# Edge features of a graph layer, by edge or by feature: four tiles per matmul, turned back through SBUF

## The reference

```python
h = maximum(layernorm(x), 0.0)                  # 6250 x 96
ea = edge_attr @ W_edge.T + b_edge              # 106250 x 96
msg = relu(h[src] + ea)                         # gather by source node
aggr = segment_sum(msg, dst)                    # scatter-add to 6250 nodes
h = (1.0 + eps) * h + aggr
h = relu(h @ W1.T + b1)
out = x + h @ W2.T + b2
```

## Time and profile before

| | before |
|---|---|
| median of 3 runs | 1239.65 us (1236.34 to 1239.94) |
| profiled execution, its span | 1239.1 us |
| its own time less the span | 0.55 us, if the median stands for it: no time of its own is given |
| TensorE matmul, weight load busy | 628.9, 515.6 us |
| VectorE, ScalarE busy | 518.5, 193.0 us |
| GpSimd busy | 785.9 us |
| bytes moved by DMA | 93.30 MB, mean 75 GB/s |

### The profile page before, as it was taken

The page is one execution under the profiler, slowest core; times in us unless marked ns, Lnnn a source line. Parts: engine busy times, 40 slices in busy tenths (PEclk is TensorE's granted clock), DMA queues, the critical chain, the costliest instruction groups (busy, mean ns, idle before and its releaser), DMA issues.

```text
span 1239.1 us, 9124 instructions
## 1 busy us (share of the span) xinstructions
PE 628.9 (51%) x2786; PEld 515.6 (42%) x2786; DVE 518.5 (42%) x658; ACT 193.0 (16%) x233; POOL 785.9 (63%) x838
## 2 busy tenths in 40 slices
PE   2226544455554454555554555444555545554568
PEld 2215434344433334444444444343444434443456
DVE  6645344444433333354344333333343444333373
ACT  5102111111111111111111111111111111111114
POOL 6756666666666666666666666666666666666540
PEclk9999666665656665565665656655556565565668
DMA  8513222333222223333333332222222333232212
GB/s 217 145 33 94 66 64 67 74 85 74 67 67 67 68 67 75 72 73 75 74 93 95 76 74 66 67 67 67 64 66 68 74 88 72 68 67 61 49 29 78
DMA packets 51183, 93.30 MB, mean 75 GB/s; under 512 B 17722, under 2 KB 20443, under 8 KB 51136
## 3 DMA queue, kind: packets, MB, share of 16 engines
q0 software_dynamic: 26592, 40.85, 16.3%
q1 hardware_dynamic: 24390, 51.63, 15.2%
q10 hardware_dynamic: 154, 0.24, 0.1%
HBM read 87.85 MB, written 4.80 MB: 75 GB/s over the span
## 4 chain that ended last, share of the span: by engine, by line
another core or an unknown queue 56%; DVE 23%; issue 8%; DVEq 8%; PE 3%; DMA 1%; ACT 0%; SPq 0%; ACTq 0%
DVE edge_ps L854 7%; DVE edge_ps L865 5%; DVE msg_parts L879 4%; DVEq L768 3%; DVE acc L759 2%; DVEq L770 2%; DVE acc L849 1%; PE edge_ps L601 1%; DVEq L762 1%; DVE stats L639 1%; PE edge_ps L462 1%; DVEq L795 1%; DVE select L705 1%; DVEq L783 1%
## 5 line engine op out<-in xcount | busy, mean ns | idle before, releaser
L352 POOL DMA_INDIRECT gathered<-h_table,src_all x810 | 764.5, 944 | 396.4 <-issue 234.7
L462 PE MATMUL edge_ps<-w_edge,edge_in 97*128 97x96 f32 x1660 | 403.6, 392 | 521.4 <-issue 517.1
L462 PEld LDWEIGHTS edge_ps<-w_edge,edge_in 97*128 97x128 f32 x1660 | 361.8, 302 | 565.0 <-issue 564.1
L787 DVE TENSOR_REDUCE sums<-agg_ps 128x192 f32<-128x576 f32 x41 | 31.0, 757 | 590.4 <-remote 590.4
L424 ACT ACTIVATE msg_parts<-edge_ps 128x960 bf16<-128x960 f32 (+1 forms) x83 | 79.2, 957 | 970.1 <-DVE edge_ps L865 704.4
L543 PE MATMUL agg_ps<-msg_parts,select 128*128 128x288 bf16 x816 | 167.9, 386 | 6.4 <-issue 6.4
L705 DVE TENSOR_TENSOR select<-const_ps,dst_rel 128x2560 bf16<-128x2560 f32 (+1 forms) x43 | 120.8, 2812 | 34.8 <-issue 28.5
L543 PEld LDWEIGHTS agg_ps<-msg_parts,select 128*128 128x128 bf16 x816 | 109.4, 134 | 60.9 <-issue 8.1
L865 DVE TENSOR_TENSOR edge_ps<-edge_ps,gathered 128x960 f32<-128x960 f32 (+1 forms) x83 | 90.9, 1141 | 47.9 <-remote 42.8
L854 DVE SCALAR_TENSOR_TENSOR edge_ps<-edge_ps,msg_parts 128x960 f32<-128x960 f32 (+1 forms) x83 | 91.1, 1144 | 0.3 <-issue 0.3
L879 DVE TENSOR_TENSOR msg_parts<-edge_ps,msg_parts 128x960 bf16<-128x960 f32 (+1 forms) x83 | 90.8, 1136 | 0.3 <-issue 0.3
(11 more groups left out here) (73 smaller groups left out, 143.1 us busy)
## 6 DMA issues: line engine op xcount, KB each, us to landing
edge_in<-edge_t_dram SPq DMA_DIRECT2D x165, 240.0 KB
gathered<-h_table,src_all POOLq DMA_INDIRECT x810
x_all<-x_dram SPq DMA_DIRECT2D x5, 420.0 KB
h_all<-x_dram SPq DMA_DIRECT2D x10, 210.0 KB
out_dram<-h_all SPq DMA_DIRECT2D x10, 210.0 KB
h_table<-h_all SPq DMA_DIRECT2D x3, 420.0 KB
h_table<-h_all SPq DMA_DIRECT2D x1, 630.0 KB
dst_by_row<-dst_rows_dram SPq DMA_DIRECT2D x1, 480.0 KB, 4.2
```

The source lines that it names most:

```text
L352: nc.gpsimd.indirect_dma_start(out=gathered[c % SLOTS][:, at:at + D], out_offset=None, in_=table, in_offset=bass.IndirectOffsetOnAxis(ap=s ...
L462: mm = pe.matmul(edge_bank(c, g)[:, (k - k0) * D:(k - k0 + 1) * D], edge_in[c % SLOTS][:, k * EDGE_TILE:(k + 1) * EDGE_TILE], w_edge[:], s ...
```

## The change

For the 40 batches 1 to 40 the edge features are made by feature: `w_edge` is the loaded operand (97 x 96), and the moving operand is four edge tiles side by side (97 x 512). Five matmuls make a batch, each filling one PSUM bank with 96 features by 512 edges. The fifth bank is `prep_ps`, which the base transposes and the tail use as well. ScalarE then copies the batch out of PSUM into `edge_blocks` in SBUF, 32 partitions at a time: twelve copies of 32 x 640 put each 32 x 32 block where its turned one belongs. VectorE turns all the blocks with two transposes of 128 x 960 back into PSUM, and from there all goes on as before. `put_base` moves ahead of `sum_windows` on VectorE, and the tail's matmul gets its own place on TensorE.

```diff
+        edge_blocks = sb("edge_blocks", [128, MOST * D])
-        edge_ps = [psum(f"edge_ps{p}", [128, 2 * BANK]) for p in range(PAIRS)]
+        turn_ps = psum("turn_ps", [128, (2 * PAIRS + 1) * BANK])
+        edge_ps = [turn_ps[:, 2 * p * BANK:2 * (p + 1) * BANK] for p in range(PAIRS)]
+        prep_ps = turn_ps[:, 2 * PAIRS * BANK:(2 * PAIRS + 1) * BANK]
         agg_ps = psum("agg_ps", [128, SIDES * BANK])
-        prep_ps = psum("prep_ps", [128, BANK])
...
+            def move_blocks(c):
+                edges = turn_ps[:, 0:tiles_of[c] * EDGE_TILE].rearrange("f (t e) -> f t e", e=EDGE_TILE)
+                blocks = edge_blocks[:, 0:tiles_of[c] * D].rearrange("e (t f) -> e t f", f=D)
+                act.wait_ge(edge_done, c + 1)
+                if c > 1:
+                    act.wait_ge(edges_turned, turned_to[c])
+                for e in range(0, EDGE_TILE, TURN):
+                    for f in range(0, D, TURN):
+                        last = nc.scalar.copy(blocks[e:e + TURN, :, f:f + TURN], edges[f:f + TURN, :, e:e + TURN])
+                last.then_inc(blocks_moved, 1)
...
+                if by_feature(c + 1):
+                    move_blocks(c + 1)
...
+            def edge_features_by_feature(c):
+                loaded = 0
+                for q, k0 in enumerate(range(0, tiles_of[c], TURN_TILES)):
+                    k1 = min(k0 + TURN_TILES, tiles_of[c])
+                    while loaded * GROUP_TILES < k1:
+                        pe.wait_ge(edges_in[c % SLOTS][loaded], 16 * loads_to[c][loaded])
+                        loaded += 1
+                    if q == 2 * PAIRS:
+                        if c > 1:
+                            pe.wait_ge(blocks_moved, c - 1)
+                        if c > BASE_FROM:
+                            pe.wait_ge(base_put, min(c - BASE_FROM, BASES))
+                        if c == TAIL_AT + 1:
+                            pe.wait_ge(tail_added, 1)
+                    elif q % 2 == 0:
+                        pe.wait_ge(low_made, adds_to[c - 1] + q // 2 + 1)
+                    mm = pe.matmul(turn_ps[0:D, q * BANK:q * BANK + (k1 - k0) * EDGE_TILE], w_edge[:],
+                                   edge_in[c % SLOTS][:, k0 * EDGE_TILE:k1 * EDGE_TILE], start=True, stop=True)
+                    if q == 0:
+                        mm.then_inc(edge_begun, 1)
+                mm.then_inc(edge_done, 1)
...
                 pe.wait_ge(base_put, k)
+                pe.wait_ge(blocks_moved, BASE_FROM + k)
...
+            def turn_blocks(c):
+                dve.wait_ge(blocks_moved, c)
+                for p, (k0, k1) in enumerate(pairs[c]):
+                    for a, b in pieces(c, k0, k1):
+                        last = nc.vector.transpose(in_flat(c, a, b), flat_rows(edge_blocks, a, b))
+                    last.then_inc(edges_turned, 1)
...
-                dve.wait_ge(edge_done, c + 1)
+                if by_feature(c):
+                    dve.wait_ge(edges_turned, turned_to[c + 1])
+                else:
+                    dve.wait_ge(edge_done, c + 1)
...
-                if c >= 1:
-                    if 0 < c - BASE_FROM <= BASES:
-                        dve.wait_ge(base_put, c - BASE_FROM)
-                    sum_windows(c - 1, *bounds)
                 if 0 <= c - BASE_FROM < BASES:
                     put_base(c - BASE_FROM)
+                if c >= 1:
+                    if 0 <= c - BASE_FROM < BASES:
+                        dve.wait_ge(base_put, c - BASE_FROM + 1)
+                    sum_windows(c - 1, *bounds)
...
+                if by_feature(c + 1):
+                    turn_blocks(c + 1)
```

More of the change, by code:

```diff
@@ L39 @@
 TAIL_AT = 18
+TURN = 32
+TURN_TILES = 4
 X_FROM = 17
@@ L102, in gnn_layer, with by_feature @@
     assert len(pairs[LAST - 1]) < PAIRS == len(pairs[LAST - 2])
+    assert TURN_TILES * EDGE_TILE == BANK and D % TURN == 0 and EDGE_TILE % TURN == 0
+    assert MOST <= (2 * PAIRS + 1) * TURN_TILES and tiles_of[END] <= 2 * PAIRS * TURN_TILES
     spread = engine_spread(NP)
+    turned_to = [sum(len(pairs[b]) for b in range(1, c)) for c in range(LATE + 1)]
+    def by_feature(c):
+        return 1 <= c < LATE
     h_table = nc.dram_tensor("h_table", (N, D), F32, kind="Internal").ap()
@@ L200, in gnn_layer @@
         edge_done = sem("edge_done")
+        blocks_moved = sem("blocks_moved")
+        edges_turned = sem("edges_turned")
         added = sem("added")
@@ L253, in in_banks, with in_flat, flat_rows @@
             return edge_bank(c, k0 // GROUP_TILES)[:, 0:(k1 - k0) * D].rearrange("e (t d) -> e t d", d=D)
+        def in_flat(c, k0, k1):
+            if k1 - k0 == PAIR_TILES:
+                return edge_ps[k0 // PAIR_TILES][:].rearrange("e (h c) -> e h c", h=2)[:, :, 0:GROUP_TILES * D]
+            return edge_bank(c, k0 // GROUP_TILES)[:, 0:(k1 - k0) * D]
+        def flat_rows(rows, k0, k1):
+            if k1 - k0 == PAIR_TILES:
+                return rows[:, k0 * D:k1 * D].rearrange("e (h c) -> e h c", h=2)
+            return rows[:, k0 * D:k1 * D]
         def in_rows(rows, k0, k1):
@@ L451, in _, with tail_edge_features @@
         def _(pe):
+            def edge_features_by_feature(c):
[19 more added lines that the diff above has]
+                mm.then_inc(edge_done, 1)
+            def tail_edge_features():
+                pe.wait_ge(tail_in, 16)
+                pe.wait_ge(base_put, BASES)
+                pe.wait_ge(blocks_moved, TAIL_AT)
+                pe.matmul(tail_ps, edge_tail_in[:], w_edge[:], start=True, stop=True).then_inc(tail_edge_done, 1)
             def edge_features(c):
@@ L466, in edge_features @@
                             mm.then_inc(edge_begun, 1)
-                if c == TAIL_AT:
-                    pe.wait_ge(tail_in, 16)
-                    pe.wait_ge(base_put, BASES)
-                    pe.matmul(tail_ps, edge_tail_in[:], w_edge[:], start=True, stop=True).then_inc(tail_edge_done, 1)
                 mm.then_inc(edge_done, 1)
@@ L561, in _ @@
                     turn_base(c - BASE_FROM)
+                if c == TAIL_AT:
+                    tail_edge_features()
                 if c == LAST:
@@ L573, in _ @@
                         pe.wait_ge(ones_copied, 1)
-                    edge_features(c + 1)
+                    if by_feature(c + 1):
+                        edge_features_by_feature(c + 1)
+                    else:
+                        edge_features(c + 1)
             sum_late_windows(LAST)
```

## The result

The changed kernel takes 1224.91 us (median of 4 runs, 1223.61 to 1225.26) against 1239.15 us for the kernel before in the same comparison: a ratio of 0.9892, 95% interval 0.9877 to 0.9907, so 1.1% faster. I had forecast 1262 us, 1.8% slower. The profiled execution has a span of 1223.1 us, 16.0 less than the 1239.1 before.

The account below looks back on a forecast made before the run. Gathers plus the release behind them were taken to bound the kernel, with the data path slack. On 1239.65 us, loop 0, start +10 and end +12 gave 1262 us; range 1150 to 1345.

Parts of the forecast that it names:

- Gathers plus release: Loop: 20 gathers take 24.6 us, then a 3.81 us wait for held TensorE completions; the period is 28.46 us.
- The data path after the release: Steady batch: edges 7.6, moves 9.6, turning 2.2, add to middle 6.6 us; 26.0 us, below the 28.46 us period.
- the edges' term: TensorE: 8 of a batch's 10 edge records are left after the release, 7.6 us where 5.98 stood.
- The moves: ScalarE: twelve copies per batch at 0.80 us, 9.6 us on the data path; low end 5.0, high end 16.7.
- The transposes: VectorE: two transposes of 128 x 960 per batch take 2.22 us; high end 4.4.
- The loop: Steady batches: the gathers keep the period at 28.46 us and cover the longer data path; change 0.
- Case A: Likeliest, chance 0.34: loop locked at 28.46 us by the gathers, the ends pay; 1262 us, own range 1250 to 1275.
- case B: Chance 0.34: 34 load-and-matmul pairs per period instead of 64 let the release come sooner; about 1190 us.
- The start: Before GpSimd's restart at 98.95: moves and turns add 11.8 us, all on the path; sum +10, ends -13 and +13.
- case D: Chance 0.12: no change; the start escapes the hold (-13), the end pays +12, the loop is locked; 1239 us.
- The end: Last, shorter batches: gathers no longer cover the data cycle of 26.8 us; +4 and +8, sum +12, low end 0.
- The removed weight loads: TensorE: 8.61 us of weight loads lie under 8.82 us of matmuls per batch; their going is priced at nothing.

Follow-up runs that it names:

- before_10: The kernel before with 10 gathers per batch instead of 20 in batches 2 to 39: 729.4 us, ratio 0.590.
- few_sums: The changed kernel with 4 sum matmuls per batch instead of 20: 1264.42 us, ratio 1.0184.
- split20: The changed kernel with 20 edge matmuls of 128 columns per batch instead of five of 512: 1255.2 us, ratio 1.0171.
- half_rows: The changed kernel with gathers of 64 rows instead of 128 in batches 2 to 40: 1223.22 us, ratio 0.988.
- split10: The changed kernel with 10 edge matmuls of 256 columns per batch instead of five of 512: 1350.02 us, its traced run 1320.05 us.

## Why the prediction was wrong

**What bounds the kernel: right.** "Gathers plus release" is what every run shows. From the first to the last restart 766 gathers are issued (37 batches of 20, 16 and 10): 1092.8 us before, 1.427 each, and 1084.8 us after, 1.416 each. The change moved the loop by that hundredth of a microsecond.

**The data path after the release: over-sized, by the edges' term.** I added 7.6 us for the eight records that would follow the release. They had all been computed while their completions were held, so the moves start 0.14 us after the reduction (630.82 and 630.68); the term is 0.1. The moves took 8.31 us and not 9.6 (0.682 us each, where the line through the earlier trace rows gave 0.80; with the twelve moves of 512 elements in batch 40, 0.575 each, the slope is 0.84 ns per element and the fixed part 0.15 us). The Trainium skill ("Perfetto Trace Analysis", section "Optimizing Scalar/DVE Operations") has that fixed part small, about 51 ns; that was nearer than my 0.39, which came from activations of 96 elements. The transposes took 2.25 as taken. From release to the end of the middle it is 591.65 - 574.19 = 17.5 us, not 26.0. VectorE's idle before the reduction is therefore 10 to 15 us and not 2 to 4.

**The loop: right in kind, 8 us off.** Case A had it locked at 28.46; it is 28.4 in the batches with base transposes and 28.25 in those with double windows. The mechanism of the double window was not among my rivals: GpSimd passes from one batch to the next without a wait when the first edge matmul has been let through in time, and pays the constant 0.5 us once for two batches. My case B, a release that comes sooner because there are fewer pairs, is refuted: in before_10 the release follows the halved gathers with all 64 pairs in place, and few_sums, with 18 pairs a batch, still has edges held for 15.5 us (1106.1 to 1121.6) and takes 1.43 us per gather over the three batches shown.

**The start: the step that failed.** I held on to "the release would be at 89.2" and put the 11.8 us of moves and turns behind it: "Sum +10, all of it on the path". Measured is -6.7: the moves and turns are not on the path at all. The changed kernel's start:

```profile
56.43 6.52 PE L505 MATMUL turn_ps<-edge_in,w_edge 97*96 97x512 f32 x10 [8.46 <-issue]
...
62.99 8.31 ACT L451 COPY edge_blocks<-turn_ps 32x640 f32<-32x640 f32 x12 [6.83 <-issue]
...
84.89 7.64 PE L505 MATMUL turn_ps<-edge_in,w_edge 97*96 97x512 f32 x10 [3.04 <-issue]
```

The ten records of batch 1 get past the hold at once (62.99), the 40 of the kernel before don't (92.27); the whole data path of batch 1 then runs under the gathers, and the restart at 92.24 is set by them alone. This was the low end of my term, -13, which I kept for case D at 0.12; and -13 was itself 6 us too low, since it let GpSimd restart at the end of its last gather. The release at 89.2 was the 3.5 us behind 20 gathers, while 41 run in a row at the start: 34.43 + 1.40 x 41 + 0.5 = 92.3. split20 shows the other side: with 40 records the restart is at 110.31, where my step had 109. So the path was right for the case that I chose, and the choice was wrong; that the numbers agree so well is partly luck, since a release 3.4 us too early and moves 1.3 us too long offset each other. Why ten records pass and 40 do not, no row of before could tell, and it stays open.

**The end: +12 forecast, -1.1 measured.** It rested on a data path of 26.8 us against windows of 22.84 and 14.52. With 17.5 us, and with the windows of batches 40 and 41 run together, the stretch takes 37.57 us for 37.36; the rest, -1.3, is mostly the clock. split20's 42.48 shows what a held batch costs there.

**The removed weight loads: no gain of their own.** PEld fell from 515.6 to 249.7 us. The ten records stream in 6.5 to 7.6 us where 40 took 8.82, but a single window is 28.5 us with the 64 pairs of the kernel before and 28.4 with the 34 of the changed one, so this is not where the time came from. split20, with the same loaded operand and four times the instructions, is 30 us slower.

The sign of the forecast hung on two terms, start and end, 22 us in all; they came out at -7.8, and the loop, which is nearly all of the run, at -8.2. Nothing of the gain was forecast by the case that I took.

## What to carry to other kernels

When a stretch is set by something that no row of the change touches, price the change at its ends first: that is where a covered data path comes into the open. Where the low end of a term rests on whether a wait applies at all, give it a case with a chance from its count (ten instructions or 40), not a bound in a range. And try the same edit with the cover taken away: with half of the gathers the change costs 294 us, which the 1.1% gain does not tell.

## What the runs showed of the hardware

- An indirect gather of 128 rows has GpSimd busy for 0.94 us and is issued every 1.25 us, but costs 1.40 us of something behind it. With 64 rows it is busy for 0.90 us, and the cost behind is the same. The window is 1.40 n + 0.5 us for 10, 16, 20, 40 and 41 gathers. It is not the moving of data that lasts so long: the gathers' last packet ends 1.3 us after the last gather on GpSimd, and then the DMA engines are idle for 5.6 us before the restart (double windows; 7.3 in half_rows). While it lasts TensorE can be down to one instruction every 1.40 us (split20's start).
- While that backlog lasts, completions of TensorE reach other engines late, by 9 us in the double window above (last record's end 621.82, release 630.7), by 23 us in split10's start (64.4 to 87.4) and by 27 in split20's (65.4 to 92.6). Those of VectorE and ScalarE do not in the loop (in the double window the transposes start 0.03 us after the moves end at 582.63). VectorE's own have an exception at the start: in the kernel before, the select at 69.09 waits 6.34 us for `dst_rel`, which VectorE itself has written by 62.76. The Trainium skill ("Perfetto Trace Analysis", section "Per-instruction lifecycle: what the profiler-reported window actually captures") says that phases such as the propagation of semaphores lie outside the window that a record shows; the trace agrees, and here they are longer than the window.
- At the start few TensorE instructions get through at once where many are held: ten record pairs of fp32 matmuls, not 20 or 40, with the same columns and the same loaded operand.
- What resource it is, and why it lets the first instructions of a window pass, stays open. No run separates the gathers' packets from their completion updates: none has gathers without an update, or the same number of gathers with fewer packets. Nor does any run tell whether the taking of the profile has a part in it.
